# A four-layer convolution block: GpSimd's share of the middle convolutions and of the variance stage moved to other engines

## The reference

```python
x = x + L0(gn(x))     # convolutions 3x3 (q, k, v) and 7x7, attention inside each channel
x = x + L1(gn(x))     # 3x3 convolution of values rounded to -127..127 with one scale for the tensor
x = x + L2(gn(x))     # depthwise 3x3, its kernels generated from each sample's channel means
x = x + L3(gn(x))

# L1
s = max(abs(t)); q = clip(round(t * (127 / s)), -127, 127)
out = conv3x3(q, qw) * (s * sw / 127**2) + bias
# L2
kernels = (relu(x.mean(axis=(2, 3)) @ w1 + b1) @ w2 + b2).reshape(16, 32, 3, 3)
# L3
avg, avg_sq = pool3x3(x), pool3x3(x * x)
lstd = sqrt(maximum(avg_sq - avg * avg, 1e-6))
mn, mx = lstd.min(axis=(0, 2, 3)), lstd.max(axis=(0, 2, 3))
lstd = (lstd - mn) / (mx - mn + 1e-8)
out = maximum(conv21x21(x, centre[b % 8]) - lstd * conv21x21(x, surround[b % 8]), 0)
```

## Time and profile before

| | |
|---|---|
| time, median of 3 runs | 1413.55 us (1412.29 to 1417.16) |
| profiled execution: own time | 1413.83 us |
| profiled execution: span | 1412.0 us |
| mean granted TensorE clock | 0.879 of full speed |
| PE busy | 1170.5 us (83%) |
| PEld busy | 796.3 us (56%) |
| DVE busy | 893.7 us (63%) |
| ACT busy | 560.6 us (40%) |
| POOL busy | 573.7 us (41%) |

### The profile page before, as it was taken

The page is one execution under the profiler, slowest core; times in us unless marked ns, Lnnn a source line. Parts: engine busy times, 40 slices in busy tenths (PEclk is TensorE's granted clock), DMA queues, the critical chain, the costliest instruction groups (busy, mean ns, idle before and its releaser), DMA issues.

```text
span 1412.0 us, 38547 instructions
## 1 busy us (share of the span) xinstructions
PE 1170.5 (83%) x16376; PEld 796.3 (56%) x16376; DVE 893.7 (63%) x1103; ACT 560.6 (40%) x722; POOL 573.7 (41%) x463
## 2 busy tenths in 40 slices
PE   0489999999999999992354486599988999999897
PEld 0478999999999999992211243111113444444343
DVE  5444657575858574737699487799984455435353
ACT  4643455545455545332352485355541111111010
POOL 2045464646464746453164586488870000000000
PEclk9989999999999999997666599655558999999998
DMA  7302020202010101000011133000024454554554
GB/s 103 70 2 66 3 64 4 58 10 54 14 47 22 36 3 35 4 3 1 27 52 46 34 111 86 16 0 0 0 74 102 109 143 133 143 133 111 145 138 93
DMA packets 130232, 81.04 MB, mean 57 GB/s; under 512 B 95761, under 2 KB 119602, under 8 KB 129074
## 3 DMA queue, kind: packets, MB, share of 16 engines
q1 hardware_dynamic: 130098, 78.99, 22.4%
HBM read 36.42 MB, written 11.99 MB: 34 GB/s over the span
## 4 chain that ended last, share of the span: by engine, by line
PE 44%; SPq 20%; DVE 16%; issue 10%; POOL 3%; ACT 3%; DMA 3%; DVEq 1%; POOLq 0%; ACTq 0%
PE psum L1427 35%; SPq L486 12%; SPq L475 3%; SPq L493 3%; DVE small L819 2%; DMA edge_columns<-arena 2%; ACT arena L1061 2%; POOL arena L1335 2%; PE psum L1455 2%; PE psum L1447 2%; DVE arena L915 1%; DVE arena L909 1%; DVE arena L831 1%; DVE arena L922 1%; DVE small L925 1%
## 5 line engine op out<-in xcount | busy, mean ns | idle before, releaser
L1427 PE MATMUL psum<-arena 128*128 128x64 f16 (+2 forms) x11904 | 513.5, 207 | 43.6 <-ACT arena L1061 40.5
L1427 PEld LDWEIGHTS psum<-arena 128*128 128x128 f16 x11904 | 496.6, 99 | 59.1 <-issue 40.8
L607 DVE TENSOR_TENSOR arena<-psum,arena 128x512 f32<-128x512 f32 x128 | 87.6, 690 | 196.9 <-PE psum L1427 168.1
L1620 PE MATMUL psum<-arena 128*128 128x480 f16 (+2 forms) x960 | 196.5, 366 | 3.6 <-DVEq L122 2.0
L1271 POOL TENSOR_TENSOR arena<-arena 128x256 f16<-128x256 f32 x64 | 51.3, 801 | 326.6 <-ACT arena L1055 326.6
L1620 PEld LDWEIGHTS psum<-arena 128*128 128x128 f16 x960 | 94.2, 98 | 104.6 <-issue 5.1
L1632 PE MATMUL psum<-arena 128*128 128x512 f16 x576 | 133.2, 392 | 17.7 <-DMA arena<-edge_columns 17.7
L1275 POOL TENSOR_SCALAR arena<-arena,constants_f 128x256 f16<-128x256 f16 x128 | 138.3, 1108 | 0.0
L1051 ACT ACTIVATE arena<-arena 128x256 f16<-128x256 f32 x64 | 26.7, 417 | 228.6 <-issue 127.8
L1632 PEld LDWEIGHTS psum<-arena 128*128 128x128 f16 x576 | 57.3, 101 | 91.4 <-issue 15.3
L953 DVE TENSOR_TENSOR arena<-arena 128x1024 f16<-128x1024 f32 x16 | 19.6, 1226 | 131.3 <-ACT arena L1226 131.3
(11 more groups left out here) (186 smaller groups left out, 1779.3 us busy)
## 6 DMA issues: line engine op xcount, KB each, us to landing
arena<-edge_columns SPq DMA_DIRECT2D x160, 80.0 KB
arena<-in_filter_tables SPq DMA_DIRECT2D x8, 1280.0 KB, 6.0
X<-in_x SPq DMA_DIRECT2D x64, 128.0 KB, 3.1
arena<-arena SPq DMA_DIRECT2D x32, 256.0 KB, 4.0
out<-X SPq DMA_DIRECT2D x64, 128.0 KB, 2.5
arena<-arena SPq DMA_DIRECT2D x48, 132.0 KB, 2.5
arena<-arena SPq DMA_DIRECT2D x32, 140.0 KB, 2.6
arena<-arena SPq DMA_DIRECT2D x16, 280.0 KB, 2.7
```

The costliest lines, as they stand in the source:

```text
L607: v.tensor_tensor(out_, bank_rows(k), biasrow, ALU.add).then_inc([g.staged0, g.staged1][k], 1)
L1427: last = mm(conv[k][:, c0:c1], win[:, kk, lx, y + e, dx:dx + W, :].rearrange("p w s -> p (w s)"), wt[:, lw, d, w0:w1], start=(n == 0), sto ...
L1620: mm(bank[4 * s + 2 * f + hf][:, C * lo:C * hi], tb[:, f, d + 2, lt], xt[s][:, hf, lx, YP + d + lo:YP + d + hi].rearrange("p y c -> p (y c)"),
```

## The change

What it does:

- **Constants.** The float16 identity `unit16` is replaced by `over`, which adds the rows of partitions of another group to the first or last group.
- **Layer 0's end.** The bias of layer 1 is added to x with the attention result; the statistics that layer 1 uses are corrected for it.
- **Layer 1.** `dequantise` and GpSimd's `add1` are gone: VectorE adds to x straight from PSUM, with the scale as a factor (`add1`, L899). The clamp of the last 32 partitions goes to GpSimd (`clamp1`, L1371). VectorE's loop is written out, 19 turns in which the addition and the statistics of a sample come LAG = 3 turns after its rounding.
- **Layer 2.** `kv` is split into two float16 parts once. Spreading a sample's kernels is one float16 product of 768 elements, on VectorE (`spread_kernels`, L941). GpSimd keeps only the low part of 32 partitions. LAG = 3 here too; the statistics of the first nine samples (`all_stats(2)`) are taken after the addition of sample 8.
- **Memset.** GpSimd clears the whole area of the variance stage, 12448 words per partition, in one instruction ahead of layer 1 (L1375), and pads rows then.
- **Variance stage.** The image is no longer summed over columns. It is split as it is, into a padded window `wx3`, and TensorE sums three columns and the rows: twelve products with `near` for a sample, then six with `over` from `cx3`. In `cx3` SyncE puts rows of the neighbouring groups, with four DMAs for each sample (`neighbours`, L525). The squares are summed over two columns by GpSimd and over the third by VectorE (L977); their low part is VectorE's (L983); four products, four DMAs, two products. VectorE takes the minimum and maximum of samples 0 to 7 behind their variance (EARLY = 8), and of samples 8 to 15 after `low(0, 1)` and `turn_in(1, 0)` of the filters.
- **End of the variance.** The extremes go across partitions by small copies on VectorE in place of the transposes on TensorE.
- **Filters.** `prefetch` is split, and its parts for the first turn are issued earlier, between the last steps of the variance. Edge products use 120 partitions instead of 128; the last eight were cleared before.
- **Areas.** The regions of the arena lie in another order: those for layer 2's spread kernels lie over two buffers of the filters, and the variance stage's begin behind layer 2's.

**VectorE, inside the variance stage.** Before, from the loop; L915 is the low part, L909 and L910 the row sums, L922 the variance, L924 and L925 the extremes.

The diff, cut to what the steps need:

```diff
+    to_row = np.where(p < 2 * C, G - 1, 0)
+    over = (p[None] // C == to_row[:, None]) & (p[:, None] % C == p[None] % C)
+    half = np.concatenate([ident * 4096.0, near, over], 1).astype(np.float16)
...
+            def neighbours(dst, src, done):
+                for q, r, l in ((0, 0, 0), (1, 0, 1), (2, G - 1, 1), (3, G - 1, 0)):
+                    to, of = (0, 1) if r == 0 else (1, 0)
+                    sp.dma_start(dst[C * q:C * q + C, to:to + NY - 1, :].rearrange("p y w -> p (y w)"),
+                                 src[C * r:C * r + C, l, of:of + NY - 1, :].rearrange("p y w -> p (y w)")
+                                 ).then_inc(done, 16)
+            sp.wait_ge(g.zero3, 1)
+            for n in range(B):
+                sp.wait_ge(g.xl3, n + 1)
+                neighbours(cx3[n % 2], wx3[n % 2], cx_in[n % 2])
+                if n:
+                    sp.wait_ge(g.sql3, n)
+                    neighbours(cq3[(n - 1) % 2], wq3[(n - 1) % 2], cq_in[(n - 1) % 2])
+            sp.wait_ge(g.rows_q, B)
             load_tables(0, 0)
+            sp.wait_ge(g.sql3, B)
+            neighbours(cq3[(B - 1) % 2], wq3[(B - 1) % 2], cq_in[(B - 1) % 2])
+            sp.wait_ge(g.padsB_0, 2)
+            store_edges(0, 0)
+            copy_outer(0, 0)
+            sp.wait_ge(g.s3x, B)
+            load_edges(0, 0)
+            sp.wait_ge(g.s3q, B)
+            sp.wait_ge(g.padsB_1, 2)
+            prefetch(0, 1)
             load_tables(1, 1)
...
+            def round1(n):
                 v.wait_ge(g.y1_ready, n + 1)
+                v.tensor_scalar(y12[:, n % NS], y12[:, n % NS], QMAX, MAGIC, ALU.min, ALU.add).then_inc(g.rounded, 1)
+            def clamp1(n):
                 v.wait_ge(g.rounded, n + 1)
                 v.wait_ge(g.c1_done, n - NS + 1 + free12["c1_done"])
+                v.tensor_scalar(a12[0:96, n % NS, 0, 0:NY, PAD1:PAD1 + W], y12[0:96, n % NS], MAGIC - QMAX, MAGIC,
+                                ALU.max, ALU.subtract).then_inc(g.q1_ready, 1)
+            def add1(n):
+                xb = X[:, n].rearrange("p y w -> p (y w)")
+                v.wait_ge(g.c1_done, n + 1 + free12["c1_done"])
+                v.scalar_tensor_tensor(xb, psum[:, 1024 * (n % NS):1024 * (n % NS) + 1024], one[4], xb,
+                                       ALU.mult, ALU.add).then_inc(g.x2_sum, 1)
+            for n in range(B + LAG):
+                if n < B:
+                    round1(n)
+                if n >= LAG:
+                    add1(n - LAG)
+                if n < B:
+                    clamp1(n)
+                if n >= LAG:
+                    sample_stats(n - LAG, g.x2_sum, g.x2_ready)
...
+            link(v.tensor_scalar(kv.rearrange("p v b -> p (v b)"), tp[0][:, 0:12 * B], KS, None, ALU.mult))
+            link(v.tensor_copy(kv16[:, :, 0, :], kv.rearrange("p v b -> p b v")))
+            link(v.tensor_tensor(kv16[:, :, 1, :], kv.rearrange("p v b -> p b v"), kv16[:, :, 0, :], ALU.subtract))
...
+            def spread_kernels(n):
+                v.wait_ge(g.c2_done, n - NS + 1 + free12["c2_done"])
+                v.tensor_tensor(k2[:, n % NS].rearrange("p l (v c) -> p (l v) c", c=C),
+                                kv16[:, n].rearrange("p l v -> p (l v)").unsqueeze(2).broadcast_to([P, 24, C]),
+                                unit32.unsqueeze(1).broadcast_to([P, 24, C]), ALU.mult).then_inc(g.k2_ready, 1)
...
+            def low_x(n):
+                k = n % 2
                 v.wait_ge(g.xh3, n + 1)
+                v.tensor_tensor(wx3[k][:, 1, :, PAD1:PAD1 + W], y3[k].rearrange("p (y w) -> p y w", w=W),
+                                wx3[k][:, 0, :, PAD1:PAD1 + W], ALU.subtract).then_inc(g.xl3, 1)
+            def row_squares(n):
+                k = n % 2
+                v.wait_ge(g.half_q, n + 1)
+                out_ = row_q[k].rearrange("p (y w) -> p y w", w=W)
+                v.tensor_tensor(out_, out_, sq3[k][:, :, 2:2 + W], ALU.add).then_inc(g.rows_q, 1)
+            def low_squares(n):
+                k = n % 2
+                v.wait_ge(g.sqh3, n + 1)
+                w_ = wq3[k].rearrange("p l y w -> p l (y w)")
+                v.tensor_tensor(w_[:, 1], row_q[k], w_[:, 0], ALU.subtract).then_inc(g.sql3, 1)
...
+            def variance(n):
+                k = n % 2
+                v.wait_ge(g.s3q, n + 1)
+                v.wait_ge(g.m2, n + 1)
+                v.scalar_tensor_tensor(local_var[:, n], psum[:, 2048 * k + 1024:2048 * k + 2048], 1.0 / 36.0,
+                                       local_var[:, n], ALU.mult, ALU.subtract).then_inc(g.v3, 1)
+            def extremes(n):
+                v.wait_ge(g.v3, n + 1)
+                v.tensor_reduce(lows3[:, n:n + 1], local_var[:, n], AX.X, ALU.min).then_inc(g.reduced, 1)
+                v.tensor_reduce(highs3[:, n:n + 1], local_var[:, n], AX.X, ALU.max).then_inc(g.reduced, 1)
...
+            v.wait_ge(g.x3_ready, B)
+            group_sums(3)
+            for n in range(B + 3):
+                if n >= 3:
+                    variance(n - 3)
+                    if n - 3 < EARLY:
+                        extremes(n - 3)
+                if n < B:
+                    low_x(n)
+                    row_squares(n)
...
+                if 1 <= n <= B:
+                    low_squares(n - 1)
+                if n == B - 2:
+                    turn_in(0, 0)
+                if n == B - 1:
+                    low(0, 0)
+                if n == B:
+                    turn_in(0, 1)
+            low(0, 1)
+            turn_in(1, 0)
+            for n in range(EARLY, B):
+                extremes(n)
...
+            def prepare3(n):
+                k = n % 2
+                wait_reuse(a, g.xl3, n - 1)
+                a.activation(y3[k], X[:, n].rearrange("p y w -> p (y w)"), ACT.Identity, scale=scale3[:, n:n + 1],
+                             bias=shift3[:, n:n + 1]).then_inc(g.y3_ready, 1)
                 a.wait_ge(g.y3_ready, n + 1)
+                wait_reuse(a, g.rows_q, n - 1)
+                a.activation(sq3[k][:, :, PAD1:PAD1 + W], y3[k].rearrange("p (y w) -> p y w", w=W), ACT.Square,
                              scale=2.0 / XS).then_inc(g.sqf3, 1)
+                wait_reuse(a, g.s3x, n - 1)
+                a.activation(wx3[k][:, 0, :, PAD1:PAD1 + W], y3[k].rearrange("p (y w) -> p y w", w=W), ACT.Copy
+                             ).then_inc(g.xh3, 1)
...
+            def clamp1(i, k):
+                n = NS * i + k
+                gp.wait_ge(g.rounded, n + 1)
+                wait_alone(gp, g.c1_done, n - NS + 1 + free12["c1_done"])
+                gp.tensor_scalar(a12[96:P, k, 0, 1:1 + NY, PAD1:PAD1 + W], y12[96:P, k], MAGIC - QMAX, MAGIC,
+                                 ALU.max, ALU.subtract).then_inc(g.q1_pool, 1)
+            gp.wait_ge(g.w2_placed, 1)
+            gp.memset(arena[:, sums_at:sums_end], 0.0).then_inc(g.zero3, 1)
             pad_rows(0, g.padsB_0)
...
+            for n in range(B):
+                k = n % 2
+                gp.wait_ge(g.sqf3, n + 1)
+                wait_reuse(gp, g.sql3, n - 1)
+                gp.tensor_tensor(row_q[k].rearrange("p (y w) -> p y w", w=W), sq3[k][:, :, 0:W], sq3[k][:, :, 1:1 + W],
+                                 ALU.add).then_inc(g.half_q, 1)
...
+            def sums_x(n):
+                k = n % 2
+                pe.wait_ge(g.xl3, n + 1)
+                wait_reuse(pe, g.m2, n - 1)
+                for hf in range(2):
+                    for dx in range(3):
                         for l in range(2):
+                            mm(bank[4 * k + hf], near, wx3[k][:, l, 8 * hf:8 * hf + 8, dx:dx + W],
+                               start=(dx + l == 0), stop=False, skip_group_check=True)
+                pe.wait_ge([g.cx_0, g.cx_1][k], 64 * (n // 2 + 1))
+                for hf in range(2):
+                    for dx in range(3):
+                        last = mm(bank[4 * k + hf], over, cx3[k][:, 8 * hf:8 * hf + 8, dx:dx + W],
+                                  start=False, stop=(dx == 2), skip_group_check=True)
+                last.then_inc(g.s3x, 1)
```

554 lines of the change are left out of this document (216 added, 338 removed).

## The result

The changed kernel takes 1353.71 us (median of 4 runs, 1353.01 to 1356.18), against 1414.47 (1412.29 to 1417.16). The ratio is 0.9573, with a 95% interval of 0.9551 to 0.9594: 61 us, or 4.3%, faster. The forecast was 1364, in a range of 1340 to 1393. The profiled execution took 1356.18 with a span of 1354.4, 2.5 over the median.

The account below looks back on a forecast made before the run. It read bounds by stage, with VectorE busy 147.1 of 161.0 us in the variance and TensorE 326.5 of 356.0 in the filters. 1413.8 + 8.6 - 1 - 4 - 48 - 5 = 1364.4, taken as 1364; range 1340 to 1393.

Parts of the forecast that it names:

- The memset: Before the quantised convolution: GpSimd's clearing of 12448 words holds VectorE's chain of small copies leading to the scale, +8.6 us.
- Quantised convolution: Layer 1: GpSimd's clamp taken as 2.06 us, a period of 5.3, 89 us against 89.5, rounded to -1.
- VectorE's addition runs beside it, its clamp can't: Quantised convolution: VectorE's clamp waits for GpSimd's clamp (P) to end; period 0.73 + max(1.21, P) + 0.1 + 0.73 + 1.65.
- The clamp is slow: Rival, quantised convolution: P = 3 to 4, VectorE stands behind it each turn, stage 103 to 118 us, total 1379 to 1393; chance 0.15.
- the clamp is quick: Rival, quantised convolution: P = 1.0, period 4.4, stage 74.5 us, total 1350, or 1341 without the hold; chance 0.20.
- Generated convolution: Layer 2: VectorE replaces GpSimd as bound at the same pace, 4.9 a turn; start -3, tail -1, together -4 us.
- Variance: Variance stage: periods 7.3 early, 5.6 late, TensorE at full clock; 113 us against 161.0, so -48.
- Filters: Filter stage: earlier first stores gain 5 us, later reductions cost nothing while SyncE's earlier transfers cover them; bounds -8 and +5.
- Now the stores of the first sample start some 3 before: Filters' start: SyncE's first store precedes TensorE's first filter product by some 3 us, where it started 2.5 after; part of -5.
- No hold by the memset: Rival, before the quantised convolution: GpSimd's memset doesn't hold VectorE, total 1356; chance 0.21.
- Half clock in the variance: Rival, variance: TensorE stays at 1.2 GHz, 10.3 us a sample, +10 in place of -48, total 1422; chance 0.08.
- SyncE limiting the variance: Rival, variance: DMA issues of 0.78 us make 6.2 per sample late and lengthen the loop, total 1370; chance 0.04.

Follow-up runs that it names:

- c_one_op: Changed kernel, with GpSimd's clamp of 32 partitions as one operation (subtract) instead of two, lower limit left out: 1343.09 us, ratio 0.9494.
- c_vector: Changed kernel, with the clamp of the last 32 partitions back on VectorE and nothing on GpSimd in the quantised convolution: 1352.18 us, ratio 0.9558.
- v_half: Changed kernel, with both additions of the squares' columns in the variance stage on VectorE, none on GpSimd: 1363.57 us, ratio 0.9641.
- v_early16: Changed kernel with EARLY = 16 instead of 8, all minima and maxima taken behind their variance: 1362.22 us, ratio 0.9631.
- f_out_pool: Changed kernel, with the filters' 64 output DMAs issued by GpSimd and the table load waiting for TensorE's last product with the old table: 1331.22 us, ratio 0.9417.

## Why the prediction was right, and where not

- **The memset: right.** Forecast 8.6, measured 8.7, and 8.5 come back when it goes. The held copy of L822 was the row to go by, not the two memsets that ran side by side. The rule of the Trainium skill (SBUF — State Buffer, Who interferes with whom), that the whole instruction of the one engine shuts the other out where they share a port pair, agrees with the 7.83 us of L857. By the same rule VectorE's scalings would also have to stop for the whole of GpSimd's one-input clamp. In c_one_op and in the changed kernel they stop only near its start and at its end, and pass in its middle.
- **Quantised convolution: the step that failed.** It was "VectorE's addition runs beside it, its clamp can't", and the price of the clamp. The price was 3.95 (the upper bound of 4.0 was right, the value of 2.06 was not), and the prediction's own terms make about 120 us of that: 1.2, three turns of 5.5, thirteen of 7.2 and 8.85. (Its 118 for P = 4.0 and 103 for P = 3 are each about 2 too low by those terms.) Measured were 76.5. The formula puts VectorE's clamp behind the whole of GpSimd's. But GpSimd's one-input instruction lets VectorE pass in its middle, and VectorE's clamp of a sample runs while GpSimd is still at an earlier one: the hold costs 0.26 in a turn, not 2.7. Two errors, the price and the hold, had opposite signs, and the second was larger. "The clamp is slow" was right in its condition and wrong in its consequence; "the clamp is quick" gave nearly the right number, 74.5, for a reason that was false. That the whole came out 10 us from the forecast owes something to luck.
- In that formula the ends were mispriced too. The first result waits for GpSimd's first clamp, and GpSimd's last clamp comes well behind VectorE's: that is why c_vector costs so little and c_one_op gains so much.
- Of the rule that one-input work on GpSimd is roughly line-rate (the Trainium skill, GPSIMD Engine Reference, Engine selection) this trace shows the contrary: 3.95 us for 1024 elements with two operations and 2.77 with one, where a subtraction of two tensors takes 2.00.
- **Generated convolution: right in the sum**, -4.6 for -4, without an experiment of its own. The parts are off: the start gained 1.3 and not 3, with the spread of kernels and a low part held beside GpSimd (2.74, 3.07 and 2.80 us at the start, where they take 0.94 and 1.21 free), and the turns are 4.65 apart (842.95 to 847.60), not 4.9.
- **Variance: right**, -50.2 for -48. Early turns 6.92 for 7.3, late ones 5.38 for 5.6, VectorE the bound (v_half), the clock at 0.95. The first variance came 16.3 after the stage's start for 18.5, but from the ninth to the first filter product it was 39.1 for 36, since the wait for the last copies wasn't in the sum. That the corner products of 32 rows kept the clock low before was only argued and has not been tried alone. "Within 4 us each time" was too strong: the group of 36 at 1330.67 of the kernel before took 10.81 for 7.93, so some 6 us at half clock by estimate.
- **Filters: a gain of 2 to 4 in place of 5**, and +1.5 in the profiled execution, 2.7 of which is the slow group at 1313.44. The extremes cost nothing, as said (v_early16). What failed is the step "Now the stores of the first sample start some 3 before" as a gain for the end. They do start earlier, at 991.74, 5.1 before the first filter product, and TensorE saves the 6.7 us of its first wait. But SyncE paces every turn (43.7 to 43.9 us against TensorE's 39.6), and its lead is used up in turn after turn: the last edge loads begin 324.1 us after the first filter product before and 322.9 after. The prediction read SyncE at the start of the stage and not over its length. f_out_pool shows what that queue cost: 22.5 us.
- **The rivals.** No hold by the memset: false. Half clock in the variance: false, 0.95 granted. SyncE limiting the variance: false in the turns, where VectorE has no pauses; SyncE's order of issues costs only at the end. The sum was 10.7 over the median. By the profile the convolution accounts for 12, the variance for 2, the generated convolution for 0.6, and the filters for -6.5; the profiled execution is 2.5 over the median.

## What to carry to other kernels

Before a period is multiplied by the number of turns, ask what the first result waits for and which engine is behind at the end: a slow engine costs its first instruction at the start and its backlog at the end, even where the turns hide it. When two engines hold each other, ask for which part of an instruction: where in the other's instruction a short one falls decides what it costs. And read a DMA queue over the whole stage: one that never rests bounds it, whatever the engines' busy shares say; moving sixty-four DMAs to an idle engine's queue was worth more than a third of the whole change. Clear only what is read.

## What was not expected of the hardware

- GpSimd's instructions with two tensor inputs, and its memset, held a VectorE scaling to their end (1.65 for 0.68, 7.83 for 0.24). Its one-input instruction of 32 x 1024 elements let scalings of 1024 elements pass in its middle at 0.64 to 0.69 us and held them near its start and at its end, about 0.9 us each (1.41 and 1.51 for 0.68 in c_one_op, 0.94 in each turn of the changed kernel).
- The hold works both ways: GpSimd's first clamp, with VectorE's scalings beside it, took 4.77 us in the changed kernel, where its shortest took 3.63.
- On GpSimd one operation per element took 2.77 us, two took 3.95 (3.63 at the least), and a two-tensor subtraction of the same 32 x 1024 took 2.00.
- GpSimd issued an output's four DMAs in 2.93 us, SyncE in 3.24; they land in 4.4 us instead of 2.5.
- A load of 1280 KB ahead of small DMAs on the same queue made these late: 5.0 us to land for copies inside SBUF that took 2.0 elsewhere, and 3.1 us of waiting for edge stores.
